# A routed FFN on one core: token rows by transposing the summed conditioned input, and scores and rows placed among the shared tiles

## What is computed

```python
xt = einsum('bct,bcd->bdt', x, weights[itok]).reshape(T, D)      # conditioned input
probs = softmax(xt @ gate_w); top_p, top_i = top_k(probs, 2)
for k in range(2):
    e = top_i[:, k]; pos = place of the token among those of expert e; keep = pos < cap
    buf[e, pos] = xt * keep
    h = gelu(buf @ w1 + b1); y = h @ w2 + b2 + gelu(buf @ wd) @ wu
    out += y[e, pos] * keep * top_p[:, k]
sh = gelu(xt @ sw1 + sb1) @ sw2 + sb2 + gelu(xt @ swd) @ swu
return x + out + 0.2 * sh
```

## Time and profile before

| | us |
|---|---|
| median of 3 runs | 199.3 |
| lowest, highest | 198.49, 199.55 |
| the profiled execution | 199.96 |
| its span, first to last instruction | 198.2 |

### The profile page before, as it was taken

The page is one execution under the profiler, slowest core; times in us unless marked ns, Lnnn a source line. Parts: engine busy times, 40 slices in busy tenths (PEclk is TensorE's granted clock), DMA queues, the critical chain, the costliest instruction groups (busy, mean ns, idle before and its releaser), DMA issues.

```text
span 198.2 us, 4057 instructions
## 1 busy us (share of the span) xinstructions
PE 184.4 (93%) x1425; PEld 175.6 (89%) x1425; DVE 143.5 (72%) x315; ACT 132.8 (67%) x283; POOL 121.6 (61%) x150
## 2 busy tenths in 40 slices
PE   6999999999799999999999999999997998999940
PEld 6986888997689999999999999998996997998840
DVE  4498598773845556796897899868878877899700
ACT  2267899004969109959959969978895977898400
POOL 6400008799628460582895895698998983877560
PEclk9999999999999999999999999999999999999996
DMA  5591600078924124526859839877757767842332
GB/s 157 141 346 54 215 2 0 0 227 226 298 89 115 47 66 119 201 76 242 230 55 306 228 40 290 227 121 235 237 81 250 250 76 230 225 56 30 41 43 30
DMA packets 23817, 29.25 MB, mean 148 GB/s; under 512 B 4442, under 2 KB 20564, under 8 KB 23796
## 3 DMA queue, kind: packets, MB, share of 16 engines
q1 hardware_dynamic: 19412, 23.03, 36.8%
q0 software_dynamic: 4016, 5.38, 16.9%
q10 hardware_dynamic: 368, 0.56, 1.0%
HBM read 23.92 MB, written 5.05 MB: 146 GB/s over the span
## 4 chain that ended last, share of the span: by engine, by line
PE 55%; POOL 18%; DMA 8%; DVE 5%; issue 5%; ACT 4%; POOLq 1%; SPq 1%; ACTq 0%; DVEq 0%
POOL out_rows L417 10%; PE hid_ps L924 8%; PE hid_ps L925 8%; PE hid_ps L926 8%; PE y_ps L926 7%; PE y_ps L924 7%; PE y_ps L925 7%; DMA w_raw<-in_L_ffn_w 4%; DMA gate_raw<-in_L_ffn_gate_w 3%; POOL wd_h L380 2%; PE turn_ps L1092 2%; DMA out_rows<-y_row,slot_tok 2%; POOL slot_in L403 1%; POOL count L436 1%; PE row_ps L1108 1%
## 5 line engine op out<-in xcount | busy, mean ns | idle before, releaser
L417 POOL DMA_INDIRECT out_rows<-y_row,slot_tok x24 | 45.9, 1911 | 11.5 <-issue 5.4
L669 DVE TENSOR_TENSOR hid_l<-gelu_f,hid_h 128x320 fp32r<-128x320 f32 (+1 forms) x80 | 41.2, 532 | 14.6 <-ACT hid_h L570 14.2
L924 PE MATMUL hid_ps<-xs_h,w_h 128*128 128x256 f32 (+2 forms) x128 | 38.2, 298 | 2.7 <-issue 1.6
L569 ACT ACTIVATE gelu_f<-hid_ps,bias_s 128x320 f32<-128x320 f32 x64 | 34.6, 541 | 7.9 <-DVE low_s L666 4.8
L925 PE MATMUL hid_ps<-xs_l,w_h 128*128 128x256 f32 (+2 forms) x128 | 36.6, 286 | 0.0
L926 PE MATMUL hid_ps<-xs_h,w_l 128*128 128x256 f32 (+2 forms) x128 | 36.6, 286 | 0.0
L403 POOL DMA_INDIRECT slot_in<-slot_rows,slot_src x24 | 28.4, 1183 | 13.4 <-issue 6.0
L570 ACT ACTIVATE hid_h<-hid_ps,bias_s 128x320 fp32r<-128x320 f32 x64 | 34.9, 545 | 0.0
L926 PE MATMUL y_ps<-hid_h,w_l 128*128 128x256 f32 (+2 forms) x112 | 32.2, 287 | 0.0
L925 PE MATMUL y_ps<-hid_l,w_h 128*128 128x256 f32 (+2 forms) x112 | 32.2, 287 | 0.0
L924 PE MATMUL y_ps<-hid_h,w_h 128*128 128x256 f32 (+2 forms) x112 | 32.2, 287 | 0.0
(11 more groups left out here) (210 smaller groups left out, 407.0 us busy)
## 6 DMA issues: line engine op xcount, KB each, us to landing
w_raw<-in_L_ffn_w SPq DMA_DIRECT2D x16, 1024.0 KB
x_in<-in_x SPq DMA_DIRECT2D x2, 512.0 KB, 4.6
w_raw<-in_L_ffn_sw SPq DMA_DIRECT2D x1, 1024.0 KB
slot_rows<-token_row SPq DMA_DIRECT2D x2, 512.0 KB, 3.6
out_rows<-base SPq DMA_DIRECT2D x2, 512.0 KB, 5.5
wu_raw<-in_L_ffn_wu SPq DMA_DIRECT2D x24, 32.0 KB
w_raw<-in_L_ffn_sw ACTq DMA_DIRECT2D x1, 512.0 KB
w_raw<-in_L_ffn_sw SPq DMA_DIRECT2D x1, 512.0 KB, 5.4
```

The source lines that it names most:

```text
L417: pool.indirect_dma_start(out=out, out_offset=bass.IndirectOffsetOnAxis(ap=slot_tok[0:n, e, s:s + 1].bitcast(U32), axis=0), in_=y_row[0:n, ...
L569: act.activation(gelu_f[:, j % 3, 0:n], src[:, 0:n], ACT.Gelu, bias=bias(j - 1))
L669: dve.tensor_tensor(hid_l[:, j - 1, 0:n], gelu_f[:, j % 3, 0:n], hid_h[:, j - 1, 0:n].bitcast(F32), ALU.subtract).then_inc(hid_split, 1)
L924: pe.matmul(out_ap, l_h, r_h, start=start, stop=False)
```

## The change

The second product goes. POOL adds `xct_h` and `xct_l` back together, in four sums of 128x512 into `xct_f`, a view of the memory of `base`, which is written only later. They stand on POOL behind `wu_hi_part(0, 0)` and ahead of the ranking. `make_rows(b)` transposes two token tiles out of `xct_f` with four PE transposes; it waits for the sums of its half of the tokens. All four go into `y_ps[0]`, one after the other, so each also waits until ACT has copied the rows before it.

The places move. `make_rows` 0 to 3 stand on PE behind the shared tiles 1, 2, 3 and 5 of the first half (`ROWS_AT`), and `copy_rows` 0 to 3 on ACT behind the gelus of the same tiles. `score(0)` goes into `y_ps[0]`, ahead of tile 0, `score(1)` into `row_ps`, behind tile 0, `gate_tokens` behind tile 1. The waits of the first three tiles for scores and row copies go; `shared_out` still asks for all four row copies. The four w2 chunks on ACT now stand in a row.

```diff
@@ pool, behind wu_hi_part(0, 0)
+            for h in range(2):
+                cols = slice(h * HALF, (h + 1) * HALF)
+                for k in range(KD):
+                    pool.wait_ge(xct_lo, h * KD + k + 1)
+                    pool.tensor_tensor(xct_f[:, k, cols], xct_h[:, k, cols].bitcast(F32), xct_l[:, k, cols].bitcast(F32),
+                                       ALU.add).then_inc(xct_summed, 1)
@@ act
-            row_banks = [y_ps[0], y_ps[1], row_ps, hid_ps[2]]
             def copy_rows(b):
                 act.wait_ge(rows_made, b + 1)
                 act.activation(token_row[:, 2 * b:2 * b + 2, :],
-                               row_banks[b][:, :].rearrange("p (t f) -> p t f", t=2), ACT.Copy).then_inc(rows_copied, 1)
+                               y_ps[0][:, :].rearrange("p (t f) -> p t f", t=2), ACT.Copy).then_inc(rows_copied, 1)
...
-            copy_rows(0)
-            w2_chunk(0, 0, 0)
-            copy_rows(1)
-            w2_chunk(0, 0, 1)
-            copy_rows(2)
-            copy_rows(3)
-            for c in range(CHUNKS // 2, CHUNKS):
+            for c in range(CHUNKS):
                 w2_chunk(0, 0, c)
...
             for j in range(HT):
                 gelu_tile(0, j, HALF, shared_bias)
+                if j in ROWS_AT:
+                    copy_rows(ROWS_AT.index(j))
@@ pe
             def make_rows(b):
+                pe.wait_ge(xct_summed, (b // 2 + 1) * KD)
+                if b > 0:
+                    pe.wait_ge(rows_copied, b)
                 for t in (2 * b, 2 * b + 1):
-                    ins = pe.matmul(row_banks[b][:, (t % 2) * D:(t % 2 + 1) * D], cond_diag[:, t, :], x_in[:, t, :],
-                                    start=True, stop=True)
+                    for k in range(KD):
+                        ins = pe.transpose(y_ps[0][:, (t % 2) * D + k * P:(t % 2) * D + (k + 1) * P],
+                                           xct_f[:, k, t * P:(t + 1) * P], ident[:, :])
                 ins.then_inc(rows_made, 1)
...
-            score(0)
-            make_rows(0)
-            score(1)
-            make_rows(1)
-            make_rows(2)
-            gate_tokens()
-            make_rows(3)
...
+                if h == 0:
+                    score(0)
                 for j in range(HT):
-                    if h == 0 and j < 2:
-                        pe.wait_ge(scores_copied, j + 1)
-                    if h == 0 and j == 2:
-                        pe.wait_ge(rows_copied, NT // 2)
                     hidden(h, j, 0, 0, xct_h, xct_l, cols, HALF)
+                    if h == 0 and j == 0:
+                        score(1)
+                    if h == 0 and j == 1:
+                        gate_tokens()
+                    if h == 0 and j in ROWS_AT:
+                        make_rows(ROWS_AT.index(j))
```

More of the change, by code:

```diff
@@ L154, in build @@
         wu_s = [sb(f"wu_s{i}", [P, D], F32R) for i in range(2)]
+        xct_f = base[:, :, :].rearrange("p t f -> p (t f)").rearrange("p (k n) -> p k n", k=KD)
         gelu_f = sb("gelu_f", [P, 3, HALF])
@@ L189, in build @@
         xct_lo = sem("xct_lo")
+        xct_summed = sem("xct_summed")
         rows_made = sem("rows_made")
@@ L264, in hid_bank @@
             return hid_ring(u)[j % len(hid_ring(u))]
+        ROWS_AT = (1, 2, 3, 5)
+        score_bank = [y_ps[0], row_ps]
         last_bank = [y_ps[0], y_ps[1], row_ps]
@@ L691, in copy_scores @@
                 dve.wait_ge(scores_made, h + 1)
-                dve.tensor_copy(scores[:, h * HALF:(h + 1) * HALF], hid_ps[h][0:2 * E, :]).then_inc(scores_copied, 1)
+                dve.tensor_copy(scores[:, h * HALF:(h + 1) * HALF], score_bank[h][0:2 * E, :]).then_inc(scores_copied, 1)
             xct_lo_half(0)
@@ L960, in score @@
                 for k in range(KD):
-                    pe.matmul(hid_ps[h][0:2 * E, :], gate2[:, k, :], xct_h[:, k, cols], start=(k == 0), stop=False)
-                    ins = pe.matmul(hid_ps[h][0:2 * E, :], gate2[:, k, :], xct_l[:, k, cols], start=False,
+                    pe.matmul(score_bank[h][0:2 * E, :], gate2[:, k, :], xct_h[:, k, cols], start=(k == 0), stop=False)
+                    ins = pe.matmul(score_bank[h][0:2 * E, :], gate2[:, k, :], xct_l[:, k, cols], start=False,
                                     stop=(k == KD - 1))
```

## The result

The changed kernel takes 203.89 us (median of 4 runs, 203.01 to 205.59), the kernel before 198.9 in the same comparison: a ratio of 1.0277, 95% interval 1.0176 to 1.0378. A later comparison gave 204.1 against 198.16, 1.0313 (1.0262 to 1.0364). The change makes the kernel about 3% slower, 5 to 6 us; 200.0 with a range of 198.8 to 202.0 was forecast. The profiled execution took 204.37 us, its span is 202.4 against 198.2.

The account below looks back on a forecast made before the run. PE, busy 93%, bounds the kernel, meeting the ranking path at 50.77. PE idles 3.7 us, saves 1.8, so is 1.9 later; spare 1.2 leaves +0.7: median 199.3 becomes 200.0, range 198.8 to 202.0.

Parts of the forecast that it names:

- The wait for the copy, less the saved work: PE before the second row transposes: 3.7 us idle until ACT's first copy, less 1.8 saved, so PE 1.9 later.
- two w2 splits at a pitch of 0.6 follow: DVE ahead of the logits: splits follow the score copy, reduce starts near 19.95, centred logits ready at 20.75.
- whether the sums would be done in time: POOL from 17.78: 1.2 us a sum taken; below 2.3 each they are in time for PE and cost nothing.
- rival (a): PE's clock drops to half rate at the 19.85 to 25.34 stall: 2.5 us lost, 202.5 total, chance 0.13.
- The slack of 1.2 us: PE near 50.77, waiting for ACT's weight split: 1.04 wait plus 0.16 spare, turning 1.9 later into +0.7.
- The ranking path: From the gelus on ACT through `used_raw` to POOL's ranking and the first expert's weights: shifts between -0.2 and +0.3 us.
- A first use paid earlier by the sums: POOL's first two-operand ranking instruction took 0.73, the next 0.21: if the sums pay first use, the path gets 0.5 back.
- Rival (b): POOL sums at 1.98 each plus 2.0 first use end at 27.7; PE loses 0.6 more: 200.6, chance 0.08.
- Rival (c): PE's later waits, some 3 us after 50.77, absorb the 0.7: 199.3, or 198.5; chance 0.17, of it 0.07 faster.
- the first output: PE's first shared output of the first half: near 35.3, with tiles 6 to 8 ending at 35.35; before, 33.45.

Follow-up runs that it names:

- before, first trace: The unchanged kernel, the profile the prediction was made from: profiled execution 199.96 us.
- before, again: The unchanged kernel, profiled a second time: 197.93 us, span 196.2.
- before, sums added: The kernel before plus the four POOL sums, which nothing on PE or ACT reads: 198.39 us against 197.96, ratio 1.0033.
- the change, again: The changed kernel, unaltered, measured and profiled a second time: 204.1 us against 198.16 for the kernel before, ratio 1.0313.
- without sums: The changed kernel without the four POOL sums, transposes reading the high part alone: 201.41 us against 197.96 for the kernel before, ratio 1.0195.
- gap filled: The changed kernel plus 80 small matmuls behind tile 2, where PE waits for the first row copy: 203.06 us against 197.96 before, ratio 1.0219.
- splits later: The changed kernel with DVE's first two w2 splits moved from ahead of the logits to behind gelu splits 1 and 2: 203.2 us, ratio 1.0259 to before.
- without sums, filled: The changed kernel without POOL sums, plus 66 small matmuls behind tile 2 in PE's wait: 200.09 us against 197.77 before, ratio 1.0126.
- rows later only: The changed kernel with rows behind tile 8 and the first output, two banks, copies behind all first-half gelus: 201.23 us, ratio 1.017 to before.
- rows at outputs: The changed kernel, rows behind tile 8 and first output, two banks, copies behind first-half gelus, sums earlier, DVE's first w2 splits later: 196.97 us, 0.996 to before.
- copies earlier: The changed kernel, first row copy ahead of Exp, next two behind gelu tiles 0 and 2, sums earlier, DVE's first w2 splits later: 198.24 us, 1.0006 to before.

## Why the prediction was wrong

The table sets side by side where PE starts the second half of the tokens, where it starts the first expert, and the span; the rest is the span less the start of the first expert.

| kernel | second half | first expert | span | rest |
|---|---|---|---|---|
| before, first trace | 45.44 | 73.47 | 198.2 | 124.7 |
| before, again | 45.34 | 72.08 | 196.2 | 124.1 |
| before, sums added | 45.39 | 72.13 | 196.4 | 124.3 |
| the change | 50.72 | 77.48 | 202.4 | 124.9 |
| the change, again | 50.73 | 77.48 | 200.9 | 123.4 |
| without sums | 48.65 | 75.40 | 199.7 | 124.3 |
| gap filled | 49.07 | 75.82 | 202.0 | 126.2 |
| splits later | 50.61 | 77.36 | 200.6 | 123.2 |
| without sums, filled | 47.34 | 74.10 | 198.9 | 124.8 |
| rows later only | 47.76 | 74.50 | 200.3 | 125.8 |
| rows at outputs | 44.59 | 71.33 | 194.3 | 123.0 |
| copies earlier | 44.88 | 71.62 | 197.7 | 126.1 |

Between the first two columns lie 26.7 to 26.8 us in every kernel but the first trace, whose 28.0 hold the slow weight load. So what the front loses reaches the experts in full. Against the second look at before, the change starts the second half 5.38 us later. The first three parts below add up to it, by the way the runs are chained; the fourth is why the forecast expected so little of such a delay to reach the end:

1. **The wait for the copy, less the saved work: 2.0.** The run without sums and with the gap filled stands at 47.34. This part was forecast as 1.9, with its steps at the right times.
2. **The late logits: 1.7 to 2.1.** Filled, with sums against without: 49.07 - 47.34 = 1.73; not filled: 50.72 - 48.65 = 2.07. This is the largest step that failed: the one on DVE, "two w2 splits at a pitch of 0.6 follow". I asked whether the sums would be done in time and gave them 0.69 to 1.98 us (they took 1.48), but I put what they do to the engine beside them at nothing, without a reason. The Trainium skill has it (GPSIMD Engine Reference, section 1, Specifications): GpSimd's SBUF interface is shared with VectorE, and they contend when a DVE instruction has two SBUF inputs. The traces agree: 1.27 us for two splits without sums, 2.72 and 3.08 beside them, while the reduces and the differences with one operand in PSUM are unchanged.
3. **The clock: 1.3 to 1.7.** 50.72 - 49.07 = 1.65 with the sums, 48.65 - 47.34 = 1.31 without. This was rival (a), with a chance of 0.13 and a price of 2.5. The mechanism was named and its chance was too low: the one case of a resting PE in the earlier trace rows is a rest at the end, and a wait of 2.37 us was enough here. The price was too high for this order, since the lower clock lasted 3.4 us, not five. With DVE's splits later it lasted 6.8, and there it cost 2.5: where the clock held, the second half began 22.02 us after the second group of transposes (49.07 - 27.05), and there 24.48 (50.61 - 26.13).
4. **The slack of 1.2 us that isn't there.** Where paths meet, the forecast took 1.2 off PE's delay, from the wait of 1.04 in the earlier trace rows. A second look at the same kernel has no such wait. That is the step that made 1.9 into 0.7, and it explains why the run without the other two causes is at 1.3% (0.8 to 1.8) and not at 0.35%: 2.0 us are 1.0%.

The four together: 0.7 forecast, 1.3 for the slack, 1.7 for the logits, 1.7 for the clock, 5.4 us, and 0.2 outside the span; the comparisons say 5.5 (3.5 to 7.5) and 6.2 (5.2 to 7.2). Parts 2 and 3 aren't independent, since later logits make the wait longer that lowers the clock.

Part 2 could have been seen in the trace of before. In the stretch that the rows cover POOL is idle, from 17.8 to 30.3; but in an expert period one-operand casts on POOL run beside DVE's splits:

```profile
115.20 2.79 DVE L633 TENSOR_TENSOR w_l<-w_raw,w_h 128x512 fp32r<-128x512 f32 x2
```

```profile
115.76 1.68 POOL L394 CAST w_h<-w_raw 128x512 fp32r<-128x512 f32 x2
```

Two splits took 2.79 us there, where 1.27 to 1.30 is usual. Whether the spread of the casts in the earlier trace rows comes from such meetings was not looked into.

The ranking path was given -0.2 to +0.3 for `used_raw`. It came at 33.71, 3.7 later, but it follows PE's tile 4 and ends nothing: ACT had the first expert's weights split by 49.9, before PE's second half began. My reason for a gain there was wrong too. POOL's first two-operand ranking step took 0.73 and 0.74 us in the two looks at before and 0.21 in the change, but also 0.20 in the run that has no sums, and 0.67 in the run with earlier copies, which has them. The step ahead of it varies likewise: 2.2 in both looks at before, 0.70 in the change and without sums, 2.73 with earlier copies. A first use paid earlier by the sums doesn't explain that; what does is open.

Rival (b), late sums: PE waited 0.88 for the first two, inside the later wait; it cost nothing of its own. Rival (c), a delay absorbed behind 50 us: not seen; the last column of the table varies by 3 us, but not with the front. It varies by 1.5 us between the two profiles of the change, whose fronts are equal, so a part of it belongs to the single execution: those of the filled run and of the run with earlier copies took 1.0 and 1.4 us more than their medians. By the medians, and with the front as profiled, the rest is 123.7 to 125.3, an estimate. What moves it is not settled; why PE waited 1.71 us for `y_row` at 144 in the filled run I did not try. It also leaves open why the run with earlier copies has no gain from a front that is 0.46 sooner; 0.2 of it goes outside the span, as in every kernel with the sums.

Two slips of my sums: 0.7 either way of 200.0 ends at 200.7, not 200.8, and the first output comes at 35.3, not 35.35. Neither changes the outcome.

## What to carry to other kernels

Before work is put on an idle engine, price what it does to its neighbour: sums of two SBUF operands on POOL more than doubled DVE's differences of two SBUF operands here, casts of one operand did so in one stretch too, and the harm depends on what stands on DVE in that stretch, not on whether the result is in time. A bank through which several steps go one after the other ties PE to the queue of the engine that empties it; the copy has to stand ahead of that engine's long work, or the step behind it. And a wait seen in one execution is a slack only if it is in a second one.

## What was not expected of the hardware

- Two DVE subtractions of 128x512 took 1.27 us alone and 2.58 to 3.08 beside POOL sums; one of 128x64 took 0.23 alone, 0.74 to 0.97 beside them. With one operand in PSUM they kept their 1.27. The four sums took 5.88 to 5.96 us, and 5.01 where DVE had less beside them.
- A PE wait of 2.37 us lowered the granted clock to half; waits of 0.68 to 1.04 did not. At half, 512 columns took 0.43 us, and the lower clock lasted 3.4 us in four profiles and 6.8 with the splits later, so that a gap that ended 1.0 sooner brought 0.1.
- The same weight load, issued within 0.1 us of the same time and with nothing changed, landed at 47.2 in one execution and at 45.0 in another.
- Every kernel with the POOL sums spends 0.2 us more outside the span from its first to its last instruction.
